# Another order for all calls of the attention part of a one-core decoder layer

## The reference

```python
x = layernorm(x + self_attention(x))        # 16 heads of 64, causal
x = layernorm(x + cross_attention(x, ctx))  # 16 heads of 8, masked, with biases
x = layernorm(x + mixture(x))               # 8 experts of width 256, top 2 of a router

h = silu(x @ w_gate[e].T) * (x @ w_up[e].T)           # for each expert e
out = out + dense_w[:, e:e + 1] * (h @ w_down[e].T)
```

## Time and profile before

| | us |
|---|---|
| median of 3 runs | 233.37 (233.29 to 233.5) |
| profiled execution | 233.06 |
| its span, first to last instruction | 231.0 |
| TensorE busy | 225.9 (98%) |
| TensorE's weight loads busy | 205.9 (89%) |
| VectorE busy | 192.1 (83%) |
| ScalarE busy | 164.9 (71%) |
| GpSimd busy | 102.0 (44%) |

### The profile page before, as it was taken

One profiled execution on the slowest core, in us unless ns is written; L12 is line 12 of the kernel. 1 busy time (PEld: TensorE's weight loads), 2 busy tenths in 40 slices (PEclk: granted clock), 3 DMA queues, 4 the chain that ended last, 5 costly groups with the idle time before them and its releaser, 6 DMA issues.

```text
span 231.0 us, 6982 instructions
## 1 busy us (share of the span) xinstructions
PE 225.9 (98%) x2274; PEld 205.9 (89%) x2274; DVE 192.1 (83%) x954; ACT 164.9 (71%) x552; POOL 102.0 (44%) x162
## 2 busy tenths in 40 slices
PE   8999999999999999999999999999999999999992
PEld 8999888997978988978978988789999999999992
DVE  3897798997889889989899879989898565766984
ACT  3768988898999979999989999697476333333001
POOL 4387738796396568922978351231200000100112
PEclk9999999999999999999999999999999999999999
DMA  6998000000000000000002200000000000000000
GB/s 189 362 363 314 10 0 0 4 3 1 3 1 3 0 6 3 0 3 1 1 4 64 121 3 3 3 0 4 0 3 0 1 3 0 4 23 0 26 23 24
DMA packets 7011, 9.10 MB, mean 39 GB/s; under 512 B 1088, under 2 KB 5824, under 8 KB 6592
## 3 DMA queue, kind: packets, MB, share of 16 engines
q1 hardware_dynamic: 4320, 7.09, 8.7%
q10 hardware_dynamic: 2656, 1.57, 2.3%
HBM read 8.14 MB, written 0.52 MB: 37 GB/s over the span
## 4 chain that ended last, share of the span: by engine, by line
PE 96%; DVE 1%; issue 1%; POOL 1%; ACT 0%; POOLq 0%; ACTq 0%; DVEq 0%
PE bank L1545 13%; PE bank L1443 11%; PE bank L1445 10%; PE bank L1444 10%; PE bank L2043 9%; PE bank L1527 7%; PE bank L1554 7%; PE bank L1595 6%; PE bank L1563 4%; PE bank L1538 3%; PE bank L1611 2%; PE bank L1482 2%; PE bank L1483 2%; PE bank L1484 2%; PE bank L1570 2%; PE bank L2053 1%
## 5 line engine op out<-in xcount | busy, mean ns | idle before, releaser
L525 ACT ACTIVATE probs_s<-masked_s,nmax_s 128x128 f32<-128x128 f32 x128 | 49.8, 396 | 3.6 <-DVE nmax_s L839 2.1
L311 POOL TENSOR_TENSOR probs_s<-probs_s,rec_sum_s 128x512 f32<-128x512 f32 x32 | 33.1, 1040 | 35.0 <-DVE rec_sum_s L846 34.8
L586 ACT ACTIVATE silu<-bank 128x256 f32<-128x256 f32 x54 | 20.1, 384 | 30.3 <-PE bank L1445 28.4
L528 ACT ACTIVATE probs_c<-masked_c,nmax_c 128x128 f32<-128x128 f32 x128 | 40.3, 396 | 1.6 <-DVE nmax_c L839 1.4
L1443 PE MATMUL bank<-ctx_hi,gu_hi 128*128 128x256 f32 x128 | 38.7, 302 | 0.0
L1444 PE MATMUL bank<-ctx_lo,gu_hi 128*128 128x256 f32 x128 | 35.7, 279 | 0.0
L1445 PE MATMUL bank<-ctx_hi,gu_lo 128*128 128x256 f32 x128 | 35.7, 279 | 0.0
L839 DVE CUSTOM_DVE_ANT_0 masked_c<-bank,mask_add 128x128 f32<-128x128 f32 x128 | 29.0, 286 | 4.6 <-PE bank L1538 3.9
L839 DVE CUSTOM_DVE_ANT_0 masked_s<-bank,causal 128x128 f32<-128x128 f32 x128 | 29.2, 285 | 1.2 <-PE bank L1527 1.0
L503 POOL TENSOR_TENSOR mv<-mv,minus_half 128x1 f32<-128x1 f32 x7 | 3.8, 556 | 55.2 <-DVE mv L1388 55.2
L1443 PEld LDWEIGHTS bank<-ctx_hi,gu_hi 128*128 128x128 f32 x128 | 24.3, 190 | 0.7 <-DVE qk_a L969 0.3
(11 more groups left out here) (180 smaller groups left out, 591.4 us busy)
## 6 DMA issues: line engine op xcount, KB each, us to landing
raw<-in_gateT SPq DMA_DIRECT2D x1, 1024.0 KB, 8.2
raw<-in_upT SPq DMA_DIRECT2D x1, 1024.0 KB, 12.1
down_sb<-in_down SPq DMA_DIRECT2D x1, 1024.0 KB, 5.2
raw<-in_wvT SPq DMA_DIRECT2D x1, 512.0 KB, 5.6
ctxT_all<-in_ctxT SPq DMA_DIRECT2D x1, 512.0 KB, 6.9
masked_c<-in_mask ACTq DMA_DIRECT2D x1, 512.0 KB, 11.9
wo_sb<-in_woT SPq DMA_DIRECT2D x1, 512.0 KB, 6.1
x_tok<-in_x ACTq DMA_DIRECT2D x1, 512.0 KB, 11.2
```

The costliest lines, as they stand in the source:

```text
L311: pool.tensor_tensor(probs_s[:, g % 2], probs_s[:, g % 2], spread(rec_sum_s[:, 4 * g:4 * g + 4], 2, S), ALU.mult).then_inc(normed[g], 1)
L525: last = act.activation(probs_s[:, g % 2, i, :], masked_s[:, g % 2, i, :], ACT.Exp, scale=-1.0, bias=nmax_s[:, h:h + 1], accum_out=rsum_s[ ...
L528: last = act.activation(probs_c[:, g % 2, i, :], masked_c[:, g % 2, i, :], ACT.Exp, scale=-1.0, bias=nmax_c[:, h:h + 1])
L586: act.activation(silu[:, i % NS, :], g, ACT.Silu).then_inc(silued, 1)
```

## The change

All lists of the attention part, on all engines, stand in another order, up to the 31st gate_up; the banks are given out anew (the arguments of the calls, Y_BANK, MAIN_BANK and FILL_BANK), and the explicit waits on TensorE follow from that. No call is added or removed: 285 calls on TensorE before and after, five explicit waits fewer. Most calls are a few places off from where they were.

The head of the diff, then the parts that concern the argument (TensorE at batches 6 and 7, and the end of VectorE's list):

```diff
-        Y_BANK = [X0, OC, T0]
-        MAIN_BANK = [Y0, OS, X1, Y1]
+        Y_BANK = [X0, OC, Y0]
+        MAIN_BANK = [T0, T1, Y1, X1]
...
-        FILL_BANK = [OC, OC, X0, OS, OC, T1, Y0, X0, OC, X1, Y0, OS, X1, Y0, OS, T0,
-                     T1, Y0, X0, T1, X1, Y1, OC, T0, X0, Y0, OS, OC, X1, Y1, T0, T1]
+        FILL_BANK = [OS, Y0, X0, X0, OC, Y0, T1, X0, OS, T1, T0, OS, T1, T0, OS, X1,
+                     Y1, T0, OS, X0, T1, Y1, X1, Y0, X0, T0, T1, OC, Y1, X1, Y0, OS]
...
 # GpSimd
             split_x(0)
             split_x(1)
             round_ctx(0)
-            split_x(2)
-            split_x(3)
             normalise(0, 0)
...
+            own_k(0)
+            split_gu(0)
+            own_k(1)
+            split_x(3)
...
 # TensorE, batch 7
             gate_up(5)
-            pe.wait_ge(maxed["c"][0], 8)
-            gate_up(6)
             pe.wait_ge(maxed["c"][1], 8)
             turn_x2(4, T0)
-            pe.wait_ge(res2_done, 6)
-            turn("c", 0, 7, X0)
-            pe.wait_ge(logit_evac, 4)
-            turn("c", 1, 7, OC)
-            route(4, T0)
-            turn_oc(6, Y1)
+            turn("c", 0, 7, OC)
+            gate_up(6)
+            pe.wait_ge(x2T_evac, 5)
+            turn("c", 1, 7, T0)
+            turn_oc(6, X1)
+            mix_c(0, 7, OC)
+            mix_c(1, 7, OC)
+            pe.wait_ge(maxed["c"][2], 8)
+            route(4, Y1)
+            pe.wait_ge(ccat_done, 7)
             turn_x2(5, X1)
-            pe.wait_ge(turned_evac["c"][0], 8)
+            turn_ccat(6, OS)
             gate_up(7)
-            turn_ccat(6, OS)
-            pe.wait_ge(turned_evac["c"][1], 8)
+            project_out_c(6, T0)
             gate_up(8)
-            project_out_c(6, OS)
-            pe.wait_ge(logit_evac, 5)
-            turn("c", 2, 7, T0)
-            mix_c(0, 7, Y1)
-            mix_c(1, 7, Y1)
-            turn("c", 3, 7, T1)
+            turn("c", 2, 7, Y0)
             pe.wait_ge(x2T_evac, 6)
+            turn("c", 3, 7, X1)
             gate_up(9)
...
 # TensorE, the 32 gate_up calls
             gate_up(16)
-            route(7, OS)
+            route(7, T1)
             gate_up(17)
+            pe.wait_ge(hid_done, 15)
             gate_up(18)
+            gate_up(19)
+            pe.wait_ge(logit_evac, 8)
+            gate_up(20)
             pe.wait_ge(hid_done, 17)
-            gate_up(19)
-            gate_up(20)
             gate_up(21)
             gate_up(22)
             gate_up(23)
-            pe.wait_ge(hid_done, 19)
+            pe.wait_ge(hid_done, 20)
             gate_up(24)
             gate_up(25)
+            pe.wait_ge(hid_done, 21)
             gate_up(26)
+            gate_up(27)
+            pe.wait_ge(hid_done, 22)
+            gate_up(28)
             pe.wait_ge(hid_done, 23)
-            gate_up(27)
-            gate_up(28)
             gate_up(29)
             pe.wait_ge(hid_done, 24)
             gate_up(30)
```

More of the change, by code:

```diff
@@ L1670, in _ @@
[L1670 to L1682 removed]
+            pe.wait_ge(qk_first_a, 2)
+            first_qk(5, OS)
@@ new lines, in _ @@
+            score_s(0, 0, X0, OC)
+            first_qk(6, T0)
+            next_qk(0, 0, X1)
+            first_qk(7, Y1)
+            project_v(0, 1, T1)
+            pe.wait_ge(maxed["s"][1], 1)
+            next_qk(0, 2, OC)
+            score_s(0, 1, Y0, X0)
+            project_cv(0, T0)
+            turn("s", 0, 0, Y1)
+            pe.wait_ge(qk_evac[2], 1)
+            project_cv(1, OC)
+            pe.wait_ge(qk_evac[0], 1)
+            turn("s", 1, 0, X1)
+            pe.wait_ge(maxed["s"][3], 1)
@@ new lines, in _ @@
+            project_v(0, 0, X0)
+            pe.wait_ge(turned_evac["s"][0], 1)
+            next_qk(0, 3, Y1)
+            pe.wait_ge(maxed["s"][2], 1)
+            score_s(1, 0, Y0, OS)
+            pe.wait_ge(turned_evac["s"][1], 1)
+            pe.wait_ge(cv_evac, 2)
+            score_s(1, 1, OC, X1)
+            mix_s(0, 0, Y1)
+            turn("s", 3, 0, T0)
+            pe.wait_ge(v_evac[1], 1)
+            turn("s", 2, 0, T1)
+            pe.wait_ge(cat_done[0], 1)
+            next_qk(1, 2, Y1)
@@ L1683, in _ @@
+            pe.wait_ge(v_evac[1], 2)
+            score_s(2, 0, OS, Y1)
+            mix_s(1, 0, Y0)
+            turn("s", 3, 1, X0)
+            project_v(2, 0, T0)
+            next_qk(1, 3, OC)
+            turn_x1(0, X1)
+            turn("s", 2, 1, X0)
+            pe.wait_ge(cat_done[0], 2)
+            next_qk(1, 0, Y0)
+            project_kc(1, T1)
+            project_qc(0, X1)
+            mix_s(1, 1, T0)
+            score_c(0, X0, X1, Y1, OS)
             pe.wait_ge(qk_evac[3], 2)
@@ L1863, in _ @@
-            score_s(6, 1, Y0, Y1)
-            pe.wait_ge(ccatT_evac, 4)
-            turn("s", 0, 6, T1)
+            pe.wait_ge(turned_evac["s"][1], 6)
+            score_s(6, 0, OS, Y0)
+            mix_s(5, 0, T0)
+            pe.wait_ge(maxed["c"][1], 5)
+            turn("s", 3, 5, T1)
+            pe.wait_ge(maxed["s"][1], 7)
+            turn("s", 2, 5, Y0)
+            turn_oc(3, X1)
+            project_v(5, 1, Y1)
+            pe.wait_ge(maxed["s"][0], 7)
+            next_qk(5, 1, OS)
```

963 lines of the change are left out of this document (452 added, 511 removed).

## The result

The changed kernel takes 235.5 us (median of 6 runs, 234.78 to 235.61), the kernel before 233.32 (6 runs beside them). The ratio is 1.0082, with a 95% interval of 1.007 to 1.0094: **slower by 0.8%**, outside the predicted range of 232.6 to 234.2. The profiled execution took 234.93 us, with a span of 232.9 against 231.0.

What follows compares the result with a forecast made beforehand. TensorE, busy 98% of the span, was taken to bound the kernel. Fewer changes of kind -0.5, small gaps 0 and the hidden layer +0.69 gave +0.2 us: 233.55 against 233.37, 8-in-10 range 232.6 to 234.2.

Steps and rivals of the forecast that it cites:

- Small gaps: Late TensorE starts between 104 and 155 us, 0.4 us in sum: old ones go, new ones come, net nothing.
- the sentence on GpSimd: GpSimd's queue: split_x(3) goes behind own_k(1) into idle time, is done before evac_turned("c") needs it, and costs nothing.
- Fewer changes of kind: TensorE's attention calls behind 55 us: fewer switches between tiled and whole-array calls save 0.5 us, bounds 0.3 and 0.7.
- The counts: TensorE's list: mix_c directly behind mix_c 14 times before, 16 after; tiled calls followed by whole-array calls 28, then 27.
- The hidden layer: gate_up(24) waits for hidden(19), 1.16 us; two old waits go, 0.47; net 0.69 us more, bounds +0.4 and +0.8.
- The down stretch keeps its length: From the first down projection to the end: TensorE goes at its own pace, so the length does not change.
- The faster rival: No wait at gate_up(24), both old waits gone: 232.4 us, down to 232.0 if small gaps go too; chance 0.22.
- The slower rival: VectorE, 98% busy in 120 to 130 us, cannot follow TensorE's lead: 234.05, or 234.4 with more gaps; chance 0.26.

Runs made afterwards that it cites:

- a_pool47: The changed kernel with add_out_bias(4) and (7) moved on GpSimd directly behind root(var1, 4) and (7), ahead of the products; ratio to the kernel before 1.0039.
- a_half3: a_pool47 with GpSimd's normalise(0, 3) split into two products of 256 columns; route(7) 142.13 us behind mix_s(0, 0), against 142.41 in a_pool47.
- a_h15: The changed kernel with only hidden(15) put back ahead of evac_logits(7) and rank_0 on VectorE; gate_up(31) 10.95 us behind route(7) instead of 11.25.
- a_fill8: a_h15 with every gate_up from 24 on given the bank used eight calls back; ratio to the kernel before 1.0068.
- b_fill8: The kernel before with banks of gate_up(16) to (31) chosen so each former user lies eight calls back; ratio 1.0069.
- b_x0: b_fill8 with bank X0 at gate_up(24) instead of gate_up(29), banks seven and eight calls apart; whole 0.50 us longer than in the kernel before.
- a_top: The changed kernel with the edits of a_pool47 and a_fill8 plus normalise(0, 3) in two products; 233.14 us, ratio to the kernel before 1.0001.
- b_best: b_x0 with hidden(24) moved ahead of rank_7 to rank_9 on VectorE; ratio to the kernel before 1.0126.
- a_best: The changed kernel with the edits of a_pool47 and a_fill8, plus hidden(24) ahead of rank_7 to rank_9 on VectorE; ratio to the kernel before 1.0052.

## Why the prediction was wrong

It said 233.55 us, +0.2 in sum; the median is 235.5, and the profiled execution took 1.87 us longer than that of before. By its own steps:

- *Small gaps*, "I take **nothing**, bounds -0.4 (all gone) and +0.5 (twice as many)": **this step failed.** Three holds of normalise_x1 alone put 1.30 us into such gaps ahead of TensorE, shown by a_pool47 (1.02) and a_half3 (0.28). A few other calls are late as well: turn("s", 3, 7) starts 0.26 behind turn_ccat where before has 0.16, mix_c(1, 7) is 0.10 late where I had said 0.2, and turn_x1(7) is about 0.18 late even without the hold. What each of these waits for was not tried.
- Behind that stands the sentence on GpSimd: I followed split_x(3) alone and held the queue for covered. Of own_k(7), normalise(0, 5) and normalise(0, 3), moved to directly behind root, I asked when GpSimd would finish them, never what runs on VectorE in that time. The durations of normalise_x1 in before gave a warning: three of the eight took 0.48 to 0.59 us, each ending 0.08 us behind a GpSimd instruction. I did not read them apart.
- *Fewer changes of kind*, -0.5 (bounds 0.3 and 0.7): its size stays open. With the three holds gone route(7) stands as far behind mix_s(0, 0) as in before (142.13), so nothing of a gain is left: either the saving is smaller, or the other gaps took it. The counts came true, and of the 16 pairs of mix_c 14 take 0.57 or 0.58 us. Adding up TensorE's two lists from the usual distances does not tell the two apart, because the answer depends on what is taken for usual: with the median of each pair of neighbours in before (the shortest of after where before has no such pair) the new list is 0.08 us longer (141.65 against 141.57), with the shortest distance that the sixteen profiles have for each three calls in a row it is 0.16 shorter (140.76 against 140.92). And score_s(3, 1), which both lists were to reach within 0.04 us, comes 0.11 later in after (33.30 against 33.19 behind mix_s(0, 0)).
- *The hidden layer*, +0.69 (bounds +0.4 and +0.8): right. gate_up(31) comes 0.67 us later against route(7), gate_up(24) stands 6.20 behind route(7), and a_h15 and a_fill8 show both halves of the cause. hidden(15)'s move costs 0.30, predicted 0.34.
- *The down stretch keeps its length*: right, 51.08 us in both.
- *The faster rival* supposed that there is no wait at gate_up(24). The wait is there, so it falls.
- *The slower rival*, "VectorE cannot follow the lead", reached 234.4 and had the right sign and the wrong mechanism: VectorE was less busy in after, and it was single instructions that were held. route(7) at 165.40 lies outside the 163.3 to 164.4 that I had set as the test of the forecast.

From mix_s(0, 0) on, 1.30 us up to route(7) and 0.67 behind it make 1.97. In the two profiled executions the start-up takes 0.12 off, and the first down product starts 1.85 us later. The medians lie 2.18 us apart; the interval of the ratio, 1.007 to 1.0094, is 1.63 to 2.19 us, so 1.97 fits and the difference needs no further cause.

## What to carry to other kernels

When a list of one engine is reordered, look at what starts at the same moment on its neighbours. A step that two engines wait for sets both free together, and a long GpSimd product then falls on the short VectorE instruction that TensorE needs next: put the step that waits for that short instruction ahead of the product, or split the product. And before a buffer's wait is removed by giving it another place, follow who uses that buffer next, and the one after: in the three kernels that gave the banks out anew (a_fill8, b_fill8, b_x0) a wait that was taken away came back in part, or in more than full, at the next user of a bank.

## What was not expected of the hardware

- A VectorE instruction of 0.34 us took up to 1.08 us beside a GpSimd product of 1.04 that had started first, each time until 0.08 or 0.09 us behind its end, also at a stride of two. Nothing in the idle times ahead of it shows this; only its own duration does.
- The start-up moves by 1.0 us between executions (21.8 to 22.8 us to mix_s(0, 0)), more than most effects here. Distances from a common call repeat far better. To score_s(3, 0) the four profiles of kernels made from before have 27.97 to 28.01 us, and eight of the ten made from after 28.08 to 28.12; a_fill8 and a_top have 28.24.
- In one profile each, a distance of 2.08 us between two matmuls (b_best) was followed by about three microseconds at the lower clock, and one of 1.14 us (a_best) by none.
